# Six transformer layers with windowed attention: the second key projection and the second mixing half issued ahead of the MLP's value half

## What is computed

```python
for i in range(DEPTH):                                  # DEPTH = 6
    x = attn_layer(shift_tokens(x), Wqkv[i], q_scale[i], k_scale[i], Wo[i]) + x
    x = ffn_layer(shift_tokens(x), ln_g[i], ln_b[i], W1[i], b1[i], W2[i], b2[i]) + x
# attn_layer: q, k, v of 16 heads of 64; q and k divided by their norms, times a scale, rotated;
#   attention of each window of 32 rows over its own and the previous window; @ Wo
# ffn_layer: layer norm; hg = xn @ W1 + b1; a, gate = split(hg)
#   a * gelu(gate) @ W2 + b2
```

## Time and profile before

| | |
|---|---|
| Time, median of 3 runs | 5032.56 us (5029.35 to 5033.88) |
| Profiled execution, its own time | 5031.75 us |
| Span of the profile | 5030.0 us |
| TensorE busy | 4547.3 us, 90% |
| VectorE busy | 3756.1 us, 75% |
| ScalarE busy | 3470.0 us, 69% |
| GpSimd busy | 2201.6 us, 44% |

### The profile page before, as it was taken

How to read it: one execution, slowest core, us unless ns; L and a number is a source line. 1 busy time by engine, 2 the same in 40 slices (tenths; PEclk the granted TensorE clock), 3 DMA queues, 4 the chain that set the end, 5 groups by cost and what they waited for, 6 DMA issues and landing times. The chain is left out here.

```text
span 5030.0 us, 122883 instructions
## 1 busy us (share of the span) xinstructions
PE 4547.3 (90%) x49788; PEld 2702.9 (54%) x49788; DVE 3756.1 (75%) x5802; ACT 3470.0 (69%) x5475; POOL 2201.6 (44%) x1271
## 2 busy tenths in 40 slices
PE   5998989869999999999999599789999999999997
PEld 2333433336666666666666233256666666666664
DVE  4777777257888888888887277278888888888884
ACT  1666666437878887887877136368888787888884
POOL 1111010036656565665654010066566565656561
PEclk6999999779999999999999679789999999999998
DMA  3211220000000000000000120000000000000000
GB/s 80 42 38 28 37 41 3 2 32 10 10 6 19 2 24 2 15 10 15 10 6 2 43 46 2 32 10 10 2 15 10 15 10 15 10 2 24 2 6 9
DMA packets 70035, 87.77 MB, mean 17 GB/s; under 512 B 22532, under 2 KB 44288, under 8 KB 68864
## 3 DMA queue, kind: packets, MB, share of 16 engines
q1 hardware_dynamic: 67720, 76.41, 6.5%
q10 hardware_dynamic: 1728, 3.15, 0.4%
HBM read 65.11 MB, written 13.63 MB: 16 GB/s over the span
## 5 line engine op out<-in xcount | busy, mean ns | idle before, releaser
L1078 PE MATMUL ps<-l_wqk,l_xa 128*128 128x512 f32 x1536 | 772.7, 627 | 42.8 <-DVE l_rs L1544 42.8
L674 DVE TENSOR_REDUCE a_pm<-ps 128x1 f32<-128x512 f32 (+3 forms) x912 | 561.8, 657 | 213.1 <-PE ps L568 208.1
L1188 PE MATMUL ps<-l_yb,l_mh 128*128 128x256 f32 x3072 | 710.1, 381 | 2.5 <-issue 2.5
L772 ACT ACTIVATE a_pt<-ps 128x512 f32<-128x512 f32 x864 | 475.3, 600 | 334.1 <-PE ps L574 331.9
L1501 POOL TENSOR_TENSOR l_pn<-l_pe,l_rl 128x1024 f32<-128x1024 f32 x192 | 365.2, 1902 | 558.6 <-DVE l_rl L1582 558.5
L1188 PEld LDWEIGHTS ps<-l_yb,l_mh 128*128 128x128 f32 x3072 | 564.3, 190 | 74.7 <-issue 5.6
L1544 DVE TENSOR_TENSOR l_rs<-ps,l_tab 128x512 f32<-128x512 f32 x768 | 491.1, 681 | 0.0
L1078 PEld LDWEIGHTS ps<-l_wqk,l_xa 128*128 128x128 f32 x1536 | 276.4, 194 | 379.4 <-issue 298.4
L1492 POOL TENSOR_TENSOR l_qkn<-l_rc,l_rn 128x1024 f32<-128x1024 f32 x192 | 386.4, 2013 | 202.5 <-DVE l_rn L1562 202.5
L1484 POOL TENSOR_TENSOR l_rc<-l_rc,l_rs 128x1024 f32<-128x1024 f32 x192 | 452.0, 2354 | 44.3 <-DVE l_rs L1544 44.3
L1552 DVE TENSOR_REDUCE l_ss<-l_sq 128x16 f32<-128x1024 f32 x384 | 464.9, 1211 | 2.8
(11 more groups left out here) (225 smaller groups left out, 9054.3 us busy)
## 6 DMA issues: line engine op xcount, KB each, us to landing
l_wqk<-in_lWqkv SPq DMA_DIRECT2D x24, 512.0 KB, 4.5
scratch<-a_parts SPq DMA_DIRECT2D x12, 768.0 KB, 4.2
a_qs<-scratch SPq DMA_DIRECT2D x72, 128.0 KB
a_ks<-scratch SPq DMA_DIRECT2D x60, 128.0 KB
l_wvt<-in_lWvT SPq DMA_DIRECT2D x12, 512.0 KB, 4.9
l_wo<-in_lWo SPq DMA_DIRECT2D x12, 512.0 KB, 6.6
l_w<-in_lW SPq DMA_DIRECT2D x12, 341.0 KB, 2.8
scratch<-b_parts SPq DMA_DIRECT2D x4, 768.0 KB, 4.7
```

The costliest lines, as they stand in the source:

```text
L674: nc.vector.tensor_reduce(to, src, AX.X, ALU.max).then_inc(s1_free, 1)
L772: nc.scalar.activation(pt[:, K % 3, n - GROUPS[k][0], :], ps[:, 3 + N2 % 3, :], ACT.Exp).then_inc(s2_free, 1)
L1078: last = nc.tensor.matmul(ps[:, x, :], xa[:, u, o:o + P], wqk[:, a * INNER + x * CH:a * INNER + (x + 1) * CH], start=True, stop=True)
L1188: last = nc.tensor.matmul(ps[:, 6, 0:2 * P], mh[:, h, :], yb[:, n % 2, h, :], start=h == 0, stop=h == LH - 1, skip_group_check=True)
```

## The change

TensorE's turn: `mix(.., 1)` and the key projection leave the start of the turn. They now come at the end of the turn before, between `value_rows` and `other` (the projection first), for the same tiles as before. The query transposes now come before `ln_mean` and `ln_spread`. ScalarE's turn: `gelu` moves behind `take_mixed(.., 0)`. VectorE's turn: `take_mixed(.., 1)` moves from the start of the next turn to a place ahead of `product` and `stream`. No instruction is added or removed, and no wait is rewritten.

```diff
--- before.py
+++ after.py
@@ -1287,12 +1287,10 @@
                                 last.then_inc(N["w2_ready"], 1)
 
                             for i in turns:
-                                mix(i - 1, 1)
-                                project_qk(i + 3, 1)
+                                head_weights_at(i, 0, 0)
+                                transpose_q(i + 2)
                                 ln_mean(i)
                                 ln_spread(i)
-                                head_weights_at(i, 0, 0)
-                                transpose_q(i + 2)
                                 score(i + 1)
                                 transpose_k(i + 2)
                                 gate(i)
@@ -1306,6 +1304,8 @@
                                 project(i, 1)
                                 mix(i, 0)
                                 value_rows(i + 1)
+                                project_qk(i + 4, 1)
+                                mix(i, 1)
                                 other(i)
                                 output(i)
 
@@ -1457,10 +1457,10 @@
                                 place_p(i)
                                 deviations(i + 3)
                                 ln_deviation(i)
-                                gelu(i)
                                 take_head_weights(i, 0, 1)
                                 take_head_weights(i, 1, 1)
                                 take_mixed(i, 0)
+                                gelu(i)
                                 place_value_rows(i + 1)
 
                         program(0, BEFORE, False)
@@ -1657,7 +1657,6 @@
                                                                xb[64:P, u, o + 1:o + 1 + CH], ALU.add, ALU.add).then_inc(N["out_done"], 1)
 
                             for i in turns:
-                                take_mixed(i - 1, 1)
                                 ln_centre(i)
                                 ln_scale(i)
                                 rotate_qk(i + 3, 1)
@@ -1670,6 +1669,7 @@
                                 take_projected(i)
                                 take_mixed(i, 0)
                                 sum_qk(i + 4, 0)
+                                take_mixed(i, 1)
                                 product(i)
                                 stream(i)
```

## The result

The changed kernel takes 5201.64 us (median; 5190.27 to 5202.6) against 5030.95 us before in the same comparison: ratio 1.0339, 95% interval 1.0326 to 1.0352. It is 171 us slower; the prediction was 5182 us.

The account below looks back on a forecast made before the run. TensorE, 90% busy, was taken as the bound. Costs of 0.62 + 0.52 + 1.12 + 1.43 = 3.69 us a group, 14.8 a layer, less 2.3, times 12 gave 150 us on 5031.75: 5182 us, range 5070 to 5235.

Parts of the forecast that it names:

- The range's lower end: Whole kernel: about 5070 us, with 4.5 us a layer covered and every chain 0.3 us a turn shorter.
- The mask chain: ScalarE, first two of four turns: gelu and load behind the mixed copy delay mask and key transposes, costing 0.62 and 0.52 us.
- The mean in g2: Third of four turns: layer norm's mean, now behind query transposes and mask, delays rotation and query projection; cost 1.12 us.
- Turn out: Last of four turns, without gelu: later output delays stream, spread, rotation and query projection; cost 1.43 us.
- the discount of 2.3 us a layer: Two groups a layer, at head matrices and loop's edge: mask wait already covered, 2.3 us off (bounds nothing and 4.5).
- The gain does not come through: Rival, three gelu turns: projection and second mixing half cover gelu, TensorE's 0.92 us each goes; 4899 us, chance 0.10.
- the layer norm's waits would be covered: Rival: VectorE makes up the later mean and spread, only the mask's 1.66 us a group stays; 5084 us, chance 0.10.
- the load would be placed early: Rival, ScalarE: table load runs ahead of the mixed copy in idle time; loss 1.2 us a group, 5090 us, chance 0.05.
- the time of 5380 us: Estimate by the skill's rule: a drain of about 1.38 us per table switch in three gelu turns adds 200 us.

Follow-up runs that it names:

- the early load: Changed kernel plus a one-column gelu on ScalarE right behind the square roots, the real gelu left behind the mixed copy: 5106.25 us, ratio 1.0158.

## Why the prediction was right

**The direction and the place** were right. The waits it named are the waits that the profile shows: the mask for the last query transpose, the stream for the spread, the rotation for the query projection. The time came out 20 us above the forecast, inside the range. The range's lower end does not follow from its own terms: 12 x (14.8 - 4.5) less 0.3 us in each of 4 x 48 turns is 66 us, which gives 5098 us and not 5070. The result does not depend on it.

**The mask chain.** Forecast: mask 6.1 to 7.15, key transposes at 9.1, cost 0.62 in g0 and 0.52 in g1. Measured: mask 5.99 to 7.02, key transposes at 8.93, cost 0.44 and 0.43. The copies overlap a little more than assumed. One reading of the rows was too simple: before the change ScalarE did not go in one stretch, but stood 0.33 us ahead of the second mixed copy until TensorE had its data. The chain worked out for the changed kernel has no such wait, and its timeline has none:

```profile
1609.92 0.66 ACT L1402 ACTIVATE l_yb<-ps 128x256 f32<-128x256 f32 x2 [0.33 <-PE ps L1172]
```

That the load is the part that costs, and could be hidden, is shown by the early load (1.0158) and by gelu's move back (1.0151).

**The mean in g2.** Forecast 1.12, measured 1.33. The rotation started at 9.00 (9.06 forecast), but the query projection came at 11.85 instead of 11.57, because the scores stood for 0.96 us (see the lines of g2 above) on nothing that the profile names. The mean's wait for the mask was right: in the g2 turn without that stall (first mixing half at 1792.24) the query projection starts at 11.48, after a wait of 0.67 us for the rotation, and the cost is 1.06 us (18.61 against 17.55). The stall of the scores was not foreseen, and its cause is open.

**Turn out.** Forecast 1.43, measured 1.73: spread at 8.76 (8.6), rotation at 11.08 (10.85), projection at 13.55 (13.35). Of the 0.30 us above the forecast 0.16 are in the start of the spread and 0.23 in that of the rotation; the rest is smaller steps. The run with turn out's old end gave 54 us for this part, 1.05 us in the turn; the other 0.7 is the spread's place behind the transposes.

**The sum, and the step that failed.** The group shown costs 3.93 us against 3.69, and in the three layers behind it the same group costs 3.67 to 3.69. That closeness is partly luck: g0 and g1 cost 0.27 us less than forecast in the group shown, g2 and out 0.51 more. The term that was mis-sized is the discount of 2.3 us a layer for the head matrices and the loop's edge, which I took as covering the wait for the mask. Most of it does not exist: the layer is 295.39 - 280.76 = 14.6 us longer, next to the undiscounted 14.8, and other layers of the block 13.6 to 14.6. What there is of it stands in turn out ahead of the loop's edge, which took 19.11 us before and 20.06 after and so lost 0.95 instead of 1.73. The group with the head matrices costs 3.3 to 4.1 us, like the others. There the wait for the mask is indeed covered, but the matrices themselves now wait 1.01 us for the product, because `other` moved right ahead of them and shares their bank:

```profile
1704.42 1.13 PE L1197 MATMUL ps<-l_wo,l_wvt 64*128 64x128 f32 x8 [1.01 <-DVE l_hh L1644]
```

12 x 14.6 = 176 us would be too much, since the first and the last layer of a block lose less: from the first mixing half to the last the two blocks are 86 and 82 us longer, 168 in all, and the stretch between them 3. That is the 171 us of the time. With the discount of 28 us left out the forecast would have been 5209 us, 7 above the result instead of 20 below it.

**The rivals.** The gain does not come through in the changed kernel (5201.64 us), but it is real: with ScalarE's gelu in its old place and two turns only, it is worth 33 us. That the layer norm's waits would be covered is out: the turns in which they act, g2 and out, carry 1.33 + 1.73 = 3.06 us of the group's 3.93. That the load would be placed early is out by its row behind the mixed copy (1610.59).

**The load.** By the Trainium skill (ScalarE: Activation LUTs, section What ACT_TABLE_LOAD costs) a drain of about 1.38 us comes with each switch of tables. In the changed kernel gelu starts 0.01 us behind the load's end (1610.59 + 1.28 = 1611.87, gelu 1611.88), and the load starts 0.02 us behind the copy. The trace shows no drain beside these loads, and the time of 5380 us that would follow from it did not come.

## What to carry to other kernels

In a pipeline of strictly ordered engines, a step that is moved earlier on one engine moves every step that used to stand between two others: look not only for what it covers, but for what it had kept apart (here the value half and the next user of its bank). Work that an engine does while it waits is free only in that place; a table load moved behind the wait becomes part of the chain, and a small call of the same function ahead of the wait brings it back. Where turns differ, change the order only in those that win.

## What had not been expected of the hardware

With gelu moved in the kernel before, a wait of 2.47 us of TensorE in an otherwise dense stretch was followed by a granted clock of 0.69 over 5.55 us, and by a mixing half of 2.05 us instead of 1.14. The length of the wait alone does not decide it. In the turn ahead a wait of 2.39 us was followed by the full clock. With mean and spread moved back, one wait of 1.70 us was followed by 0.53 over 3.60 us and another of 1.70 us by the full clock. The waits of 0.65 to 0.87 us for gelu in the turns of the earlier trace rows show no dip. What an experiment adds to TensorE's waits can thus cost about twice its length in the turns where the clock falls, and a forecast that counts only the wait is too low.

In the changed kernel TensorE stood for 0.96 us inside the scores, with no releaser shown; between 1100 and 2400 us such stalls of L1150 add up to 7.7 us in 9 cases (before, to 2370 us: 0.8 us in 2), and were not explained.
